# A graph network on one core: the gathered rows of the third and fourth pass in eight half-width buffers instead of four

## Time and profile before

| | us |
|---|---|
| median of three runs (5377.9 to 5379.51) | 5378.2 |
| profiled execution | 5363.67 |
| its span in the trace | 5361.9 |
| POOL busy | 3210.7 (60%) |
| PE busy | 2806.4 (52%) |
| DVE busy | 1951.3 (36%) |
| ACT busy | 1385.4 (26%) |

### The profile page before, as it was taken

How to read it: one execution, slowest core, us unless ns; L and a number is a source line. 1 busy time by engine, 2 the same in 40 slices (tenths; PEclk the granted TensorE clock), 3 DMA queues, 4 the chain that set the end, 5 groups by cost and what they waited for, 6 DMA issues and landing times.

```text
span 5361.9 us, 59693 instructions
## 1 busy us (share of the span) xinstructions
PE 2806.4 (52%) x16706; PEld 2541.5 (47%) x16706; DVE 1951.3 (36%) x4524; ACT 1385.4 (26%) x4351; POOL 3210.7 (60%) x3366
## 2 busy tenths in 40 slices
PE   5655666665567777777775453333334333333334
PEld 5555666665556666666663332323224222222224
DVE  4544444444456555555556111111113221111224
ACT  2111111111243333333334331111112121111113
POOL 4555555555526666666665666666665666666665
PEclk6666666666658888888887555555556555555556
DMA  6655555555532222223321111111111111111111
GB/s 189 172 149 146 146 150 142 151 149 144 151 103 83 82 83 82 82 83 83 83 79 41 34 35 35 35 34 35 35 34 47 35 34 36 35 35 35 35 35 45
DMA packets 337348, 431.81 MB, mean 81 GB/s; under 512 B 99312, under 2 KB 248675, under 8 KB 336941
## 3 DMA queue, kind: packets, MB, share of 16 engines
q0 software_dynamic: 133120, 245.58, 17.5%
q1 hardware_dynamic: 203917, 182.42, 12.1%
HBM read 406.71 MB, written 21.00 MB: 80 GB/s over the span
## 4 chain that ended last, share of the span: by engine, by line
another core or an unknown queue 39%; PE 25%; issue 13%; DVE 10%; ACT 8%; POOL 3%; DMA 1%; ACTq 1%; SPq 0%; DVEq 0%; POOLq 0%
PE bank L642 13%; PE bank L655 3%; DVE same L1561 3%; PE bank L657 3%; PE bank L748 2%; ACT acc L933 2%; POOL rows L550 2%; ACT part_sum L931 1%; DVE prod L1329 1%; DVE score L1331 1%; ACT acc L935 1%; DVE prod L1327 1%; PE bank L741 1%; ACT first_only L1018 1%
## 5 line engine op out<-in xcount | busy, mean ns | idle before, releaser
L642 PE MATMUL bank<-same,rows 128*96 128x128 f32 x4992 | 1025.7, 376 | 1525.0 <-ACT acc L935 573.6
L642 PEld LDWEIGHTS bank<-same,rows 128*96 128x96 f32 x4992 | 880.1, 237 | 1655.8 <-issue 943.7
L550 POOL DMA_INDIRECT rows<-kv_table,src_idx x832 | 790.9, 951 | 709.3 <-DVE msg L1337 460.6
L550 POOL DMA_INDIRECT rows<-pair_table,src_idx x832 | 788.4, 948 | 531.5 <-remote 242.2
L933 ACT COPY acc<-bank 96x511 f32 (+1 forms) x832 | 480.0, 577 | 2365.5 <-remote 1844.8
L550 POOL DMA_INDIRECT rows<-h_table,src_idx x832 | 790.5, 950 | 424.9 <-issue 233.3
L550 POOL DMA_INDIRECT rows<-ci_table,src_idx x832 | 787.0, 946 | 408.7 <-issue 241.7
L1257 DVE TENSOR_TENSOR same<-bank,rank_col 128x512 f32<-128x512 f32 x624 | 421.1, 678 | 990.8 <-remote 621.4
L642 PE MATMUL bank<-same,msg 128*105 128x128 f32 x1664 | 389.5, 409 | 440.5 <-ACT acc L935 430.4
L1561 DVE TENSOR_SCALAR same<-iota_s,rank_col,src_hi 128x128 f32<-128x128 f32 x832 | 235.4, 360 | 896.4 <-remote 728.5
L642 PEld LDWEIGHTS bank<-same,msg 128*105 128x105 f32 x1664 | 337.2, 279 | 462.6 <-DVE same L1257 411.6
(11 more groups left out here) (171 smaller groups left out, 3139.3 us busy)
## 6 DMA issues: line engine op xcount, KB each, us to landing
first_only<-q_table SPq DMA_DIRECT2D x832, 72.0 KB
first_only<-in_attr_cols SPq DMA_DIRECT2D x104, 384.0 KB
first_only<-rank_rows SPq DMA_DIRECT2D x104, 256.0 KB
first_only<-keep_rows SPq DMA_DIRECT2D x104, 192.0 KB
rows<-kv_table,src_idx POOLq DMA_INDIRECT x832
rows<-pair_table,src_idx POOLq DMA_INDIRECT x832
rows<-ci_table,src_idx POOLq DMA_INDIRECT x832
rows<-h_table,src_idx POOLq DMA_INDIRECT x832
```

What stands on the lines that cost most here:

```text
L550: pool.indirect_dma_start(rows[:, k, j, 0:width], None, table, bass.IndirectOffsetOnAxis(ap=src_idx[:, t:t + 1], axis=0)).then_inc(rows_in ...
L642: mm = pe.matmul(out[0:nrow, here], left(j), right(j), start=(j == 0), stop=(j == TQ - 1), skip_group_check=True)
```

## The change

The same memory is seen through two views: `rows` as before and `rows_half`, eight buffers of [4, 96] numbers. Passes three and four use the second, with eight semaphores. POOL waits for the window of quad q - 8 in place of q - 4, and so may be up to seven whole quads ahead of the sum. Passes one and two keep four buffers and their waits; the count up to which a semaphore must have risen is worked out in `landed`, since the first four semaphores are used by all passes and the other four by the last two.

```diff
-        rows = sb("rows", [P, GQ, TQ, KV])
+        rows_flat = sb("rows", [P, GQ * TQ * KV])
+        rows = rows_flat[:, :].rearrange("p (b j w) -> p b j w", b=GQ, j=TQ)
+
+        rows_half = rows_flat[:, :].rearrange("p (b j w) -> p b j w", b=2 * GQ, j=TQ)
...
-        rows_in = sems("rows_in", GQ)
+        rows_in = sems("rows_in", 2 * GQ)
...
-                self.rows = n * NG * 16 * TQ
+                self.depth = GQ if n < 2 else 2 * GQ
+                self.rows = rows if n < 2 else rows_half
+
+            def landed(self, q):
+
+                b = q % self.depth
+                before = sum(len(range(b, NQ, passes[m].depth)) for m in range(self.n) if b < passes[m].depth)
+                return rows_in[b], (before + q // self.depth + 1) * 16 * TQ
...
-        def edge_pass_pool(pool, table, width, freed):
+        def edge_pass_pool(pool, s, table, width, freed):
             for q in range(NQ):
-                k = q % GQ
-                wait(pool, freed, q - GQ + 1)
+                b = q % s.depth
+                wait(pool, freed, q - s.depth + 1)
                 for j in range(TQ):
                     t = q * TQ + j
-                    pool.indirect_dma_start(rows[:, k, j, 0:width], None, table,
-                                            bass.IndirectOffsetOnAxis(ap=src_idx[:, t:t + 1], axis=0)).then_inc(rows_in[k], 16)
+                    pool.indirect_dma_start(s.rows[:, b, j, 0:width], None, table,
+                                            bass.IndirectOffsetOnAxis(ap=src_idx[:, t:t + 1], axis=0)).then_inc(rows_in[b], 16)
...
             def spread(s, q, i, k):
...
                 wait(pe, s.same_done, q + 1)
-                wait(pe, rows_in[k], s.rows + (i + 1) * 16 * TQ)
+                wait(pe, *s.landed(q))
                 wait(pe, s.copied, q - 1)
-                window(bank[2 + 2 * (k % 2)], F, at, lambda j: rows[:, k, j, 0:F], lambda j: same[:, k % 2, j, :]).then_inc(s.agg_done.sem, 1)
+                window(bank[2 + 2 * (k % 2)], F, at, lambda j: s.rows[:, q % s.depth, j, 0:F], lambda j: same[:, k % 2, j, :]).then_inc(s.agg_done.sem, 1)
```

More of the change, by code:

```diff
@@ L569, in _ @@
                 wait(pool, kv_outs[b], 16 * len(range(b, NC, 3)))
-            edge_pass_pool(pool, kv_table, KV, msg_done)
+            edge_pass_pool(pool, passes[0], kv_table, KV, msg_done)
             for b in range(2):
@@ L573, in _ @@
                 wait(pool, relu_outs[b], 16 * len(range(b, NC, 2)))
-            edge_pass_pool(pool, pair_table, PAIR, passes[1].agg_done)
+            edge_pass_pool(pool, passes[1], pair_table, PAIR, passes[1].agg_done)
             for c in range(NC):
@@ L581, in _ @@
                 wait(pool, c_outs[b], 16 * len(range(b, NC, 2)))
-            edge_pass_pool(pool, ci_table, F, passes[2].agg_done)
+            edge_pass_pool(pool, passes[2], ci_table, F, passes[2].agg_done)
             for b in range(2):
                 wait(pool, d_outs[b], 16 * len(range(b, NC, 2)))
-            edge_pass_pool(pool, h_table, F, passes[3].agg_done)
+            edge_pass_pool(pool, passes[3], h_table, F, passes[3].agg_done)
         @block.tensor
@@ L737, in turn_rows @@
             def turn_rows(q, i, k):
-                wait(pe, rows_in[k], s1.rows + (i + 1) * 16 * TQ)
+                wait(pe, *s1.landed(q))
                 wait(pe, scan_done, q - 1)
@@ L1324, in first_pass @@
                         picks(q + 1, i if k < GQ - 1 else i + 1, (k + 1) % GQ)
-                    wait(dve, rows_in[k], s0.rows + (i + 1) * 16 * TQ)
+                    wait(dve, *s0.landed(q))
                     wait(dve, q_done, q + 1)
```

## The result

| | before | after |
|---|---|---|
| median, five runs each, us | 5378.2 | 5403.64 |
| lowest to highest | 5375.65 to 5380.27 | 5402.16 to 5408.12 |
| span of the profiled run | 5361.9 | 5403.3 |

The ratio is 1.0052, 95% interval 1.0039 to 1.0064. The forecast was no change at 5377 us.

The account below looks back on a forecast made before the run. It saw no engine busy throughout and time lost in hand-overs, with POOL held by late signals for window q - 4. Forecast: 5378.2 - 1 = 5377 us, both passes' change taken as 0; own range 5366 to 5390, outer range 5100 to 5425.

Parts of the forecast that it names:

- 0 for the change of both passes: Passes three and four: the deeper buffer leaves their length unchanged, 0 us, with -274 as other end; no change given 0.34.
- The argument for a rate: Passes three and four: pauses differ in pattern but lengths agree to 0.3 us in 1186, so a rate sets them.
- debt of POOL: Passes three and four: POOL runs up 0.70 us per quad and pays it at whichever boundary it reaches.
- Rival one: Passes three and four: slack was missing, eight buffers cover late signals, 5.00 us a quad; 5104 us, chance 0.20.
- two (5217): Passes three and four: half the gain, 5.29 us a quad in place of 5.70; 5217 us, chance 0.20 including any part between.
- Taken: -1 us together: Starts and ends of passes three and four: extra quads on hand gain -1 us, bounded by one 4.9 us pause per pass.
- pauses that grow longer with depth: POOL in passes three and four: a deeper buffer makes cycles and pauses longer while the rate stays.
- the signs it named: Passes three and four: 1186 us each, remote waits fewer than 112, longer than 4.9 us, sum near 313.
- Rival three: Ends of passes three and four: node chunks wait for windows 13.3 us apart, 46 us slower, 5424 us; chance 0.26.
- The rule on repeating gaps: POOL's gaps in passes three and four: repeating gaps can mean too few buffers; by it -274 us, 5104 us.

Follow-up runs that it names:

- half4: Half-width view with four buffers and four semaphores in passes three and four, against the kernel before: 4459.18 us, ratio 0.9997, on a chip with prompt signals.
- d223: Two row buffers in passes three and four and three in pass two, against the kernel before: 4490.05 us, ratio 1.0062, prompt signals.
- d3: Three row buffers in passes three and four, against the kernel before with four: 4461.59 us, ratio 1.0000, on a chip with prompt signals.
- d2: Two row buffers in passes three and four, against the kernel before with four: 5231.67 us, ratio 0.9970, on a chip with late signals.
- mix1s: Kernel before with 64 of 128 rows per gather in pass three, two gathers per quad in pass four; late signals: 1188.9 and 616.7 us, first to last gather.
- mix2s: Kernel before with 48 of 96 numbers per row in pass three, one of four matmuls in pass four; late signals: 1187.0 and 1168.4 us, first to last gather.

## Why the prediction was wrong

**The step that held.** "I take 0 for the change of both passes": measured -0.3 and -0.6 us. The argument for a rate, several patterns of pauses and one pace, was the right one, and its reading as a debt of POOL fits the runs: 1.43 us per gather, rested at any boundary, as a wait or as a memset. Rival one (5104) and two (5217) fall with it; no depth from two to eight changed a pass by more than 1% where signals are late.

**The step that failed.** "... four quads more on hand end nothing sooner. At the end of each pass POOL has up to 20 us more in hand, but windows are waited for by node chunks there. Taken: -1 us together." I sized only what the extra rows could gain and left out where they put the sums. If POOL's pace is fixed and it stops only when it is full, the sums are always a full set of buffers behind it at its stops: at 5.70 us a quad, four more quads put each window later by 4 x 5.70 = 22.8 us against the gathers. Measured, window 195 is copied 26.5 us later in pass three and 24.1 in pass four, counted from the first gather. POOL's last quad is released by window 199, where it was by window 203, and the eight windows behind it are no longer held back by gathers: their copies start within 0.8 us of the windows' ends and come 3.9 us apart in pass three and 5.0 in pass four, where a quad took 5.70, so a part is made up. What is left is 12.8 us in pass three and 18.4 in pass four. The term was mis-sized by 32 us in the profiled pair and by 26 in the timed ones, and that is the whole miss of the timed median.

The forecast also expected pauses that grow longer with depth. Over both passes the signs it named did come: 95 remote waits in place of 112, the longest 6.7 us, and a sum near 313. But in the plain stretch the cycle stayed at six quads and a stop of 4.3 us. And "0 for both passes" was a choice between two readings that the rows before could not settle; the 0.34 it was given says so.

**Rival three** had the right sign and place, the end of the passes (priced at +46), and a wrong mechanism in part: it foresaw several signals 13 us apart behind quad 196. There is one such gap in each pass. In pass four the copies of quads 196, 197 and 198 are these (the timeline of ACT, beside the earlier trace rows):

```profile
...
5318.48 0.58 ACT L943 COPY acc<-bank 96x511 f32 x1 [4.08 <-remote]
...
5336.85 0.58 ACT L943 COPY acc<-bank 96x511 f32 x1 [17.21 <-remote]
...
5342.40 0.58 ACT L943 COPY acc<-bank 96x511 f32 x1 [4.40 <-PE bank L652]
...
```

There is one gap of 18.4 us, where before had one of 12.7, and most of the loss is already made ahead of it. Counted from the first gather of the pass, quad 196 is copied at 5318.48 - 4167.2 = 1151.3 us; before it was 5276.79 - 4143.6 = 1133.2. These 18.1 us are about what the span's end shows.

**The rule on repeating gaps** of the Trainium skill ("Perfetto Trace Analysis", section Optimization Strategy), that they can mean too few buffers, would have given 5104 by the prediction's rows. The gaps are there and POOL's buffers are full at them, but a fifth to eighth buffer did not close them: 314.2 us of remote waits in place of 313.0.

**Still open.** Why POOL has to rest 0.18 us per gather on some chips and not on others, and why the bill comes as a late signal, mostly of PE. The traces name no releaser ("remote"). Whether the limit lies in POOL or in something that its gathers pass through is not shown, only that it goes with their number and that their packets are not late. Passes one and two are slower on those chips as well (1472.6 and 1255.8 us before, against 1092.9 and 1041.2 in half4). Pass two takes 1.51 us per gather there and 1.25 in half4, so 1.43 is the figure of passes three and four and not of every gather. That the cause is the same is likely and wasn't tested.

## What to carry to other kernels

When the pauses of a producer come in different patterns but always to the same mean pace, look for a limit of the pace and not for more buffers; a filler that costs far less than its own time speaks for it (here 14.6 us for an estimated 154). Behind a producer limited in this way, that stops only when its buffers are full, each further buffer puts the consumer one step later, and a good part of that is paid at the end of every pass. Take the least depth that covers the hand-over (three here), and try it on more than one chip.

## What the runs showed of the hardware

- The same kernel took 4461 to 4465 us on some chips and 5245 to 5378 us on others, 17 to 21% more, and the runs of one series agree within 0.6%. The profile tells the two kinds apart by POOL's remote waits in passes three and four: 313.0 us in 112 waits, or none (half4).
- With two buffers and prompt signals POOL paused for 1.8 us once in 112 gathers (d223), with three or more not (d3, half4).
- On the slower kind an indirect gather of passes three and four costs 1.43 us in the long run (1.42 on the chip of d2) though it is issued in 1.25, whether it fetches 128 rows or 64, 384 or 192 bytes each (mix1s, mix2s). In the cycles looked at, its packets are moved 2.0 to 2.3 us after its start all the while.
- A signal can reach the engines that wait for it long after the instruction that raises it is recorded as ended: 15.9 us in the earlier trace rows, 0.12 us in half4.
- 64-row gathers are issued in 902 ns in the mean with prompt signals, 128-row ones in 944: issue time hardly depends on the rows.
